# An attention and mixture-of-experts layer on one core: where GpSimd issues a batch's eight row scatters

## What is computed

```python
x = L0_attn_x                                   # (16, 512, 128)
# attention, 16 heads of 8, through a rank-8 projection V, U
q = (x @ Wq.T + bq) per head; zq = q @ V        # k, v likewise
att = softmax(zq zk^T / sqrt(rank)); y = (att @ zv) @ U.T
x = layernorm(x + y @ Wo.T + bo)
# 8 experts of 128 -> 512 -> 128, the best two of each token
probs = softmax(x @ gate_w.T); scores, idx = top_k(probs, 2); scores /= sum(scores)
out = sum over the two of score * (relu(x @ w1[e].T + b1[e]) @ w2[e].T + b2[e])
x = layernorm(x + out)
```

## Time and profile before

| | |
|---|---|
| median of 3 runs | 1260.19 us (lowest 1258.29, highest 1507.58) |
| the profiled execution | 1257.38 us, its span 1255.6 us |
| busy in the span | PE 86%, DVE 78%, ACT 72%, POOL 47% |
| mean granted clock of TensorE | 0.939 of full |
| attention passes 0 to 15 | about 77 to 905 us of the span |
| packets of GpSimd's DMA queue | 4.2% of the 16 DMA engines' span, for 264 scatters |

### The profile page before, as it was taken

One profiled execution on the slowest core, in us unless ns is written; L12 is line 12 of the kernel. 1 busy time (PEld: TensorE's weight loads), 2 busy tenths in 40 slices (PEclk: granted clock), 3 DMA queues, 4 the chain that ended last, 5 costly groups with the idle time before them and its releaser, 6 DMA issues. The chain is left out here.

```text
span 1255.6 us, 24757 instructions
## 1 busy us (share of the span) xinstructions
PE 1082.8 (86%) x7711; PEld 520.5 (41%) x7711; DVE 975.3 (78%) x2117; ACT 904.2 (72%) x1177; POOL 586.5 (47%) x823
## 2 busy tenths in 40 slices
PE   3578998989889898898988999888728999999977
PEld 2222222222222222222222222222218999999952
DVE  4578888989778797887988879797146888888845
ACT  1157877778677786867878678687618999999927
POOL 1314316255271642626336263323254777777745
PEclk9989999999899998989999899899758999999989
DMA  3733133141331413223142231400012222222246
GB/s 80 235 94 90 49 101 89 54 132 42 95 92 51 126 37 106 73 67 102 43 127 69 71 97 36 122 15 19 14 51 63 69 68 69 69 69 71 66 159 257
DMA packets 105461, 104.88 MB, mean 84 GB/s; under 512 B 21608, under 2 KB 82834, under 8 KB 105376
## 3 DMA queue, kind: packets, MB, share of 16 engines
q1 hardware_dynamic: 94912, 81.88, 22.5%
q0 software_dynamic: 8448, 16.93, 4.2%
q10 hardware_dynamic: 2016, 4.98, 1.1%
HBM read 56.06 MB, written 47.39 MB: 82 GB/s over the span
## 5 line engine op out<-in xcount | busy, mean ns | idle before, releaser
L799 DVE TENSOR_REDUCE row_max<-score_ps 128x2 f32<-128x1024 f32 x512 | 618.0, 1220 | 138.9 <-PE score_ps L571 91.3
L685 ACT ACTIVATE probs<-score_ps 128x1024 f32<-128x1024 f32 x512 | 521.6, 1023 | 157.4 <-PE score_ps L553 132.6
L534 PE MATMUL av_ps<-probs,v_one 128*9 128x512 f32 x2048 | 285.2, 630 | 7.9 <-ACT probs L685 6.5
L571 PE MATMUL score_ps<-k_stack,q_stack 48*128 48x512 bf16 x1024 | 207.5, 402 | 75.2 <-ACT probs L685 57.5
L553 PE MATMUL score_ps<-q_stack,k_stack 51*128 51x512 bf16 x1024 | 205.7, 399 | 22.0 <-DVE row_max L799 15.1
L371 POOL TENSOR_TENSOR max_parts<-neg_max,zeros 32x128 bf16<-32x128 f32 x32 | 14.2, 445 | 386.9 <-ACT neg_max L623 386.9
L1096 ACT ACTIVATE w_cur<-experts 128x1156 f32 x136 | 158.5, 1167 | 37.5 <-PEq L413 17.2
L553 PEld LDWEIGHTS score_ps<-q_stack,k_stack 51*128 51x128 bf16 x1024 | 49.2, 93 | 320.4 <-issue 154.2
L1192 POOL DMA_INDIRECT y_d<-y_out,place x136 | 136.8, 1006 | 44.7 <-issue 44.7
L846 POOL DMA_INDIRECT routed_d<-rows,slot_i x128 | 125.4, 980 | 67.2 <-issue 36.9
L1053 PE MATMUL up_ps<-xt_sb,w_cur 128*128 128x128 f32 x1088 | 146.2, 278 | 0.0
(11 more groups left out here) (187 smaller groups left out, 1153.3 us busy)
## 6 DMA issues: line engine op xcount, KB each, us to landing
k_stack<-k_stack_d SPq DMA_DIRECT2D x128, 96.0 KB, 2.4
q_stack<-q_stack_d SPq DMA_DIRECT2D x128, 96.0 KB, 2.5
x_rows_sb<-routed_d SPq DMA_DIRECT2D x136, 65.0 KB
q_stack_d<-q_parts SPq DMA_DIRECT2D x32, 192.0 KB
k_stack_d<-k_parts SPq DMA_DIRECT2D x30, 192.0 KB
x_in<-L_attn_x SPq DMA_DIRECT2D x16, 256.0 KB, 3.1
q_stack_d<-q_parts SPq DMA_DIRECT2D x32, 128.0 KB
x_res<-L_attn_x SPq DMA_DIRECT2D x16, 256.0 KB, 3.1
```

The source lines that it names most:

```text
L534: last = nc.tensor.matmul(av_ps[32 * g:32 * g + V_COLS, :], v_one[n.parity][:, kb, HG * hg + g, :], probs[:, (2 * j + g // 2) % P_RING, g ...
L571: last = nc.tensor.matmul(max_bank(b, s)[:, a, :], q_stack[n.parity][at, c, g * P:(g + 1) * P], k_stack[n.parity][at, c, :], start=True, s ...
L685: nc.scalar.activation(probs[:, s % P_RING, :, :], exp_bank(b, s)[:, :, :], ACT.Exp).then_inc(S["exp_done"], 1)
L799: nc.vector.tensor_reduce(row_max[:, m // (STEPS // 2), :, m % (STEPS // 2)], max_bank(b, s)[:, :, :], AX.X, ALU.max).then_inc(S["red_done ...
```

## The change

Two of the eight scatters stood behind the split of the second half of the maxima (`split_max(b, 1)`), four behind the splits of q and k, and two behind `split_max(n1, 0)`. Now the first two stand ahead of `split_max(b, 1)`, with their four waits, and the other six right behind it, ahead of the inverse root.

```diff
-                        if cur:
-                            split_max(b, 1)
                         if prev2:
                             pool.wait_ge(S["place_out"], p2.count(1, 1))
                             pool.wait_ge(S["top_step"], p2.count(TOP_STEPS, TOP_STEPS))
                             pool.wait_ge(S["slot_step"], p2.count(SLOT_STEPS, SLOT_STEPS))
                             pool.wait_ge(S["copied"], p2.count(1, 1))
                             scatter(p2, 0, 2)
+                        if cur:
+                            split_max(b, 1)
+                        if prev2 and cur:
+                            scatter(p2, 2, 8)
                         if prev:
                             pool.wait_ge(S["mv_ready"], p1.count(QT, QT))
...
                         if proj and not is_first(b):
                             split_q(nc.gpsimd, pool, n2)
                             split_k(nc.gpsimd, pool, n2)
-                        if prev2:
-                            scatter(p2, 2, 6)
                         if nxt:
                             split_max(n1, 0)
-                        if prev2:
-                            scatter(p2, 6, 8)
+                        if prev2 and not cur:
+                            scatter(p2, 2, 8)
```

## The result

The changed kernel takes 1283.7 us (median of 4 runs, 1281.68 to 1284.57) where the kernel before takes 1261.4 in the same comparison: the ratio is 1.0183, with a 95% interval of 1.0157 to 1.0209. It is slower by some 22 us, and lies above my range. One of the four executions of the kernel before was in a slower state of the chip (1507.58 us); the ratio leaves it out.

The account below looks back on a forecast made before the run. Bound: a step 25 halt from scatters beside k's stores, with low clock, over a hidden load chain. 12 x (52.3 - 52.87) + 6.0 = -0.8 us on the median of 1260.2: 1259 us, range 1243 to 1281.

Parts of the forecast that it names:

- What bounds the kernel now: Passes 2 to 13: step 25 halt from scatters beside k's stores, low clock behind it, hidden chain to the maxima's load.
- What the change removes: Last eight steps of passes 2 to 13: halt and its low clock go, 1.3 to 4.7 us a pass.
- Ahead of `split_max(b, 1)`: Two scatters there end the split about 0.6 us later; its loads have over 1 us of cover, price nothing.
- Ahead of the inverse root: Six scatters there make the shift 2.9 us later; ScalarE waits 1.25 us at step 17, passes 2 to 15.
- What is late next: Splits, stores, stack loads and next maxima load come 2.9 us later; this chain sets passes at 51.7 to 52.9 us.
- Passes 14 and 15: No chain hides the wait for the shift there: 2.3 us and 3.7 us, together 6.0.
- (1): Profile check: no "remote" wait of VectorE and ScalarE at step 25.
- (2): Profile check: shift about 14 us behind the places; ScalarE idle 1.2 us before first `scale_out`, 2.3 and 3.7 in passes 14, 15.
- (3): Profile check: at first scores of passes 3 to 14, TensorE released by the DMA of `max_parts` after 2 to 3 us.
- (4): Profile check: 52.3 us from places to places.
- (5): Profile check: the low clock at the starts of passes and not at their ends.
- the low clock lasts: Rival: clock stays low behind TensorE's idle time at step 0, 3.4 us a pass, 1300 us in all twelve; chance 0.14.

Follow-up runs that it names:

- four behind the root: Kernel before with its run of four scatters moved behind the inverse root, and SP loading the next pass's first maxima ahead of stores' wait and stack loads: 1212.03 us.
- pairs: Changed kernel with the six scatters split: two ahead of the inverse root, two behind it, two behind `split_max(n1, 0)`: 1268.5 us, ratio 1.0074.
- six behind the root: Changed kernel with the run of six scatters behind the inverse root, ahead of the splits of q and k: 1324.9 us, ratio 1.0494.
- Spaced: Changed kernel with an unused 128x512 addition on GpSimd between each two of the six scatters: 1330.37 us, ratio 1.057.
- the first two alone: Kernel before with only its first two scatters moved ahead of `split_max(b, 1)`: 1263.12 us, ratio 1.0017.
- the load's order: SP loads the next pass's first maxima ahead of its wait for the stored parts and the stack loads; alone on the kernel before: 1258.05 us, ratio 0.9975.
- Three early: Changed kernel with three scatters, not six, ahead of the inverse root, the last three at the end of the pass: 1228.76 us, ratio 0.9752.
- four early: Changed kernel with four scatters, not six, ahead of the inverse root, the last two at the end of the pass: 1234.42 us, ratio 0.9777.
- six late: Kernel before with its last six scatters in one run at the end of the pass, behind `split_max(n1, 0)`: 1274.63 us, ratio 1.0121.
- pairs with the chain cut: Changed kernel with scatters two by two between GpSimd's other work, and SP loading the next first maxima ahead of stores' wait and stack loads: 1210.49 us, ratio 0.963.

## Why the prediction was wrong

**What bounds the kernel now:** right in its rows. The halt at step 25 is that of four scatters beside the stores (four behind the root shows it), and the low clock stands behind it. The hidden chain is there too: it binds in pairs and in six behind the root.

**What the change removes:** the end of the pass did lose the halt and its clock: the last eight steps go from 16.2 us to 11.65, and these 4.6 are within my 1.3 to 4.7. But the 12.9 and 12.5 of passes 1 and 14, from which I reckoned, are not the length without disturbance. Pass 1 had its wait for the maxima in them, and pass 14 the meeting of `x_bo` with VectorE's L731, which comes of the two scatters in front of `x_bo` and goes with them, 0.9 us. The kernel before has that meeting in pass 3 too (L731 takes 1.19 us there), and not in pass 7, where the halt had already put L731 off.

**The step that failed** is the price of the six scatters ahead of the inverse root. I tied the halt to one place, "scatters and stores of k's parts at the same time", and so gave a run of eight scatters within 12 us a price of issue time alone where there were no stores. The evidence that I used, pass 14, has a run of four without stores; the change made runs of six, 3 us behind two others, which no pass of the trace had. I bounded the cost of every other new arrangement by the nearest rows, and not this one. In the runs that price is 3.8 us in steps 8 to 15, and with the clock behind it 2.2 more in steps 16 to 23: 6.0 us a pass against the 4.6 that the end of the pass gives back.

The rule that I weighed (the Trainium skill, DMA: Bandwidth & Descriptors, "SWDGE vs HWDGE vs iDMA": the queues of a DMA engine are kept apart and served in turns) didn't decide the matter; no run here shows in which order a DMA engine serves its queues. As I read the rule, nothing would halt, here or there, beyond the transfer time of the packets. Spaced against changed shows that the halt depends on how closely GpSimd issues, and the DMA engines are busy at 0.16 in it.

**Ahead of `split_max(b, 1)`:** price nothing, which agrees with the first two alone (1.0017, with 1 inside its interval).

**Ahead of the inverse root:** 14.05 us from places to shift were forecast, 14.35 measured. The wait of 1.25 us at step 17 was not to be seen, since the halt at step 15 had already delayed ScalarE past it: the first `scale_out` begins at 478.14, 2.3 us after the shift was ready. In pass 15, where it was 3.7 by the sum, it is 2.46 (timeline of ACT), and there I was right in kind:

```profile
908.61 0.49 ACT L617 ACTIVATE rows<-res,shift,rstd 128x128 f32<-128x128 f32 x1 [2.46 <-POOL shift L878]
```

**What is late next:** the mechanism was right and hidden. In pairs, where the shift is 0.3 us later behind the places than before, the splits of q about 3.1 us, and no halt is left, the passes take 53.4 us, against the 51.7 to 52.9 of the sum; what is over is the low clock, which lasted longer than in pass 2. In the changed kernel the halt delays the scores and so the maxima that GpSimd has to split. SP had issued its last stack load by 495.06 in pass 7 and then waited for that split, 2.8 us, which is the slack that the chain of stores and stack loads had:

```profile
494.17 0.89 SPq L909 DMA_DIRECT2D q_stack<-q_stack_d  x2
497.84 3.83 SPq L902 DMA_DIRECT2D q_stack<-max_parts  x6
```

**Passes 14 and 15:** 2.3 us forecast for pass 14, 4.5 measured, the halt again ("remote", 3.5 us in its step 15).

**The checks:** (1) held for step 25 and failed in its intent, since the "remote" wait moved to step 15; (2) held for the shift and failed for the wait; (3) failed; (4) 54.3 instead of 52.3; (5) failed, the low clock is in the middle of the pass.

**The rivals:** the low clock lasts, the first one, gave the sign and part of the size, but behind a halt that it did not name. The rival that I lacked is "the halt moves with the scatters, and grows". With the runs' 3.8 and 2.2 us it gives 12 x (6.0 - 4.6) = 17 us and with pass 14 some 22, which is what was measured; that is a sum made from the measurement, not a forecast. The range's ends, 1243 and 1281, do not quite match the cases that they are said to come from (1246 and 1279); the measured time lies outside either way.

## What to carry to other kernels

Where a trace shows a wait with no releaser next to a burst of GpSimd's indirect DMAs, don't reckon the burst as free at a place that merely lacks the other traffic: price it at the new place by its length and closeness, and test it at two lengths. Spread such DMAs between other work of GpSimd, two or three at a time; here that, with the load's order, took the passes to 49.2 us, 1.0 above pass 1, which has no scatters. And look for the next bound in the same step. Three early, which holds the splits of q and k up no more than the kernel before, gained 2.5% alone and 3.1% with the load's order. Pairs, which delays those splits, gained nothing alone (1268.5), nor did the order (1258.05), and both together 4%.

## What the hardware showed that I had not expected

- Beside a run of indirect DMAs of 128 rows of 520 bytes, 1.27 us apart, three other engines that have no part in them stood still in these traced executions. Behind two others 3 us ahead: three in a row no halt, four 1.1 us of a pass's quarter, six 3.8. At 2.23 us apart six showed none.
- The halt ended 2.3 to 2.7 us behind the start of the run's last scatter in four early, changed, six late and six behind the root (499.66 to 501.92). From four to six scatters it grew by 2.75 us, about the issue time of two.
- With no others shortly ahead, four in a row gave no halt (four behind the root), and beside SP's stores of k's parts the same four gave 1.8 us (before).
- A halt of 4.4 us was followed in pass 7 of the changed kernel by about 10 us at a granted clock of 0.50, in other passes by less; one of 1.7 us by none in passes 2 to 13 of four early. A wait of 3.64 us at the start of pass 8 in pairs cost 3.0 us more of low clock in the next eight steps.
- VectorE's L731 (128x32) takes 0.19 us in pass 7 of the changed kernel and 1.15 beside a 128x512 addition of GpSimd's in pairs with the chain cut, where the last eight steps of a pass are 0.9 us longer.
